# Attention of a macaron layer on one core: B and C scaled over all 128 partitions, M as one f32 product, and two orders at the tile's joints

## The chip, the core and the metric

The kernel runs on one core of a Trainium2 chip. The metric is the device time of one execution in microseconds (us). TensorE is PE in the rows (PEld its weight loads), VectorE is DVE, ScalarE is ACT, GpSimd is POOL, SyncE is SP.

## What is computed

A layer on x of 4 x 1024 tokens of 256 channels in f32: half a mixture-of-experts block (`f1`), an attention-like block (`at`), half the same mixture block again (`f2`), each on a layer norm of its input and added to it. The change concerns the middle block alone:

```python
xBC = x @ in_proj_w.T                       # 1024 of x, 1024 of z, 64 of B, 64 of C
xc = silu(conv4(xBC[..., :1024]) + conv_b)  # causal, 4 taps, per channel
step: h = h * exp(-exp(A)) + B_t * x_t ; y_t = sum_n h[n] * C_t[n]
yg = y * silu(z)
out = (layernorm(yg) * ln_w + ln_b) @ out_proj_w.T
```

The decay exp(-exp(A)) depends on the state number n alone (the 64 values are tested for being the same for all channels; the other way of computing is in the program and not taken).

## The kernel before

The 4096 tokens go through the middle block in 8 tiles of 512 tokens (t, 0 to 7; two tiles make one batch), each of four chunks of 128 (q, 0 to 3). The scan is done by chunks: with X the convolved x of a chunk, y = M X + (decayed C) S, where M is the masked product of B and C with the decay between two tokens in it, and S, the state at the chunk's start, takes in (decayed B) X at its end.

f32 products are made of three fast ones (`product`): a value is split into a rounded part (`_hi`, type F32R) and the remainder (`_lo`), and hi·hi + hi·lo + lo·hi are added. ScalarE rounds, VectorE (or GpSimd) subtracts.

Every engine has a written-out program, a function `tile(t, par)` in each engine's block with a loop over q, and semaphores between them; the order of work is the order of these programs. Work for tile t+1 (and t+2) is spread over the chunks of tile t:

- chunk 0: `project_bc` of t+1 on TensorE gives B and C in mm_ps, ScalarE copies them to `bc`, and GpSimd's `scale_bc` (L1180) multiplies by the table of decays `tab`, four operations: three give `g` and the fourth a half of `c_twice`.
- chunk 1: `round_g` on ScalarE (L1293, four casts), then `rest_of_g` on VectorE (L1466, three subtractions). VectorE also has `add_out` (L1504) here, which adds the output projection of the chunk before to x_res. It waits for that projection and for `res_biased`, GpSimd's addition of a bias to x_res (L1251), which GpSimd does in chunk 1 behind the power for the layer norm.
- chunk 2: `decays` on TensorE (L1686): four f32 products of g[:, 1] with `upper_twice` into one bank of mm_ps (for bo, the decayed B with tokens on partitions), then 24 products of 64 x 64 on 64 partitions into the other (M). ScalarE and VectorE split bo and mask M behind it.
- chunk 3: `transpose_xn` of tile t+2, and `rest_of_xT`.

`project_x(t, par, j)` is the projection of x's channel block j (six matmuls of 512 columns) into bank j % 2 of mm_ps; blocks 2 to 7 of tile t+1 go with chunks 0 to 2 of tile t, blocks 0 and 1 of tile t+2 with chunk 3. `project_z` gives z in two halves into zy_ps, `transpose_x` brings the next chunk's convolved x into xu_ps as X; `round_X` and `rest_of_X` split it, and the next chunk begins with the product of bo and X. In xu_ps lies the output projection too, so the second four of the eight transposes of `transpose_x` wait for `add_out`:

```python
for j in tuple(range(SUB, CT)) + tuple(range(SUB)):
    if j == 0 and not (isinstance(c, int) and c < 2):
        pe.wait_ge(s["out_added"], c - 1)
```

The part of y that comes from the state takes two more matmuls a bank (L1820, L1821), but in the first chunk of a batch: `c_twice` (128 partitions) against `S_split` (on partitions 64 to 127 the rounded S, on 0 to 63 its remainder), and the remainder of C, `g1_lo[HALF:P]`, on 64 partitions.

## Time and profile before

| what | us |
|---|---|
| median of 3 runs | 1633.81 (1628.12 to 1636.24) |
| span of the profiled execution | 1630.1 |
| `f1` / attention with its prologue / `f2`, in the profile | 0 to 484 / 484 to 1148 / from 1148 |
| a tile of the attention part | about 75 |

The page gives no time of the profiled execution beside its span; the three runs lie from 2.0 below to 6.1 above that span. In rows, a line number L is that of the kernel above; "out<-in" names the tiles, "x" the count of instructions, and brackets the engine's idle time before an instruction and what ended it. Successive matmuls overlap, so that the distance between their starts, not their duration, says what one costs.

### The profile page before, as it was taken

Reading aid. Unit: us, or ns where it says so; the run is one execution under the profiler, and the core shown is the slowest. Engines: PE = TensorE matmul, PEld = TensorE weight load, DVE = VectorE, ACT = ScalarE, POOL = GpSimd, SP = SyncE. Lnnn points to the kernel's source line nnn. Section 1 sums busy time; section 2 is a strip of 40 time slices with the busy share of each in tenths; the row PEclk is TensorE's granted clock in tenths of the full one; section 3 lists DMA queues with packets and bytes.
Section 4 is the critical chain, followed back from the end, with each engine's and each line's share of the span. In section 5 each row is a group of like instructions: output and inputs, shape, how many; then the busy total and the mean of one; then the engine's idle time right before and its main releaser. Section 6 shows DMA issues by size and latency. Waiting matters only on the chain. (4 is left out here: it accounts for less than half of the span.)

```text
span 1630.1 us, 24068 instructions
## 1 busy us (share of the span) xinstructions
PE 1408.4 (86%) x7430; PEld 1203.1 (74%) x7430; DVE 900.3 (55%) x2136; ACT 712.2 (44%) x1168; POOL 982.9 (60%) x1026
## 2 busy tenths in 40 slices
PE   6869999999926789999998999997597899999994
PEld 5758888888814667777776777776576788888883
DVE  5655323645446676676767576654476342255544
ACT  4323444444304455554545555543343244444430
POOL 2678447737455476676758576732147753773746
PEclk9989999999967789998999999899589899999997
DMA  9936667767343001000000000000712565777743
GB/s 370 388 108 217 212 219 258 268 230 266 120 151 102 1 1 30 23 27 14 27 14 28 14 27 1 27 27 1 290 53 97 197 228 201 262 252 248 262 149 123
DMA packets 90245, 225.46 MB, mean 138 GB/s; under 512 B 16640, under 2 KB 28928, under 8 KB 89216
## 3 DMA queue, kind: packets, MB, share of 16 engines
q1 hardware_dynamic: 65536, 156.64, 27.0%
q0 software_dynamic: 24576, 67.14, 12.6%
q8 instruction: 72, 1.18, 0.3%
q14 instruction: 61, 0.50, 0.1%
HBM read 114.67 MB, written 109.05 MB: 137 GB/s over the span
## 5 line engine op out<-in xcount | busy, mean ns | idle before, releaser
L374 POOL DMA_INDIRECT xg<-f_xn,f_rows x256 | 253.7, 991 | 185.5 <-issue 70.9
L401 POOL DMA_INDIRECT f_gbuf<-yg,f_rows x256 | 264.6, 1034 | 155.6 <-DMA yg<-f_yo 78.6
L809 PE MATMUL f_gu_ps<-f_wgu,f_xT 128*128 x1408 | 333.0, 379 | 0.0
L809 PEld LDWEIGHTS f_gu_ps<-f_wgu,f_xT 128*128 128x128 f32 x1408 | 253.8, 190 | 27.2
L840 PE MATMUL f_y_ps<-f_wd,f_hT 128*128 (+1 forms) x960 | 241.7, 380 | 4.9 <-DVE f_hT L636 4.8
L840 PEld LDWEIGHTS f_y_ps<-f_wd,f_hT 128*128 128x128 f32 x960 | 181.7, 190 | 32.6 <-issue 8.3
L628 DVE TENSOR_TENSOR f_h<-f_gu_ps,f_sg 128x256 f32<-128x256 f32 x176 | 74.6, 424 | 232.8 <-ACT f_sg L441 232.4
L428 ACT COPY f_xT<-f_xT_ps 128x512 f32<-128x512 f32 x232 | 136.0, 586 | 119.6 <-PE f_xT_ps L777 107.9
L654 DVE SCALAR_TENSOR_TENSOR f_xin<-f_gbuf,f_w,f_xin 128x256 f32<-128x256 f32 x256 | 124.1, 485 | 60.0 <-DMA f_gbuf<-yg,f_rows 53.1
L441 ACT ACTIVATE f_sg<-f_gu_ps 128x256 f32<-128x256 f32 x176 | 67.6, 384 | 201.0 <-PE f_gu_ps L809 201.0
L451 ACT COPY f_yo<-f_y_ps 128x512 f32<-128x512 f32 x176 | 103.2, 586 | 91.4 <-PE f_y_ps L840 91.4
L777 PE MATMUL f_xT_ps<-ident,f_xq 128*128 128x128 f32 x704 | 106.7, 275 | 34.8 <-DMA f_xq<-xg 31.8
L814 PE MATMUL f_gu_ps<-f_xT,f_wgu 128*128 128x256 f32 x512 | 130.6, 413 | 3.8 <-DVE f_hT L632 3.8
L1492 DVE SCALAR_TENSOR_TENSOR at_xs<-at_raw,at_taps,at_xs 128x512 f32<-128x512 f32 x132 | 113.9, 865 | 13.0 <-POOL at_xs L1210 9.4
L814 PEld LDWEIGHTS f_gu_ps<-f_xT,f_wgu 128*128 128x128 f32 x512 | 104.8, 210 | 20.0 <-issue 4.4
L1243 POOL TENSOR_TENSOR at_S_split<-at_S,at_S_split 64x1024 fp32r<-64x1024 f32 x32 | 77.6, 2425 | 53.1 <-ACT at_S_split L1389 53.1
L777 PEld LDWEIGHTS f_xT_ps<-ident,f_xq 128*128 128x128 f32 x704 | 82.9, 142 | 35.9 <-DMA f_xq<-xg 32.1
L1718 PE MATMUL at_xu_ps<-at_wout,at_ynT_hi 128*128 128x256 f32 x512 | 106.8, 308 | 2.4 <-DVE at_ynT_lo L1501 2.4
L1209 POOL TENSOR_SCALAR at_tap<-at_raw,at_taps 128x512 f32<-128x512 f32 x60 | 99.1, 1652 | 6.0
L636 DVE COPY f_hT<-f_hT_ps 128x256 f32<-128x256 f32 x176 | 74.5, 423 | 40.4 <-PE f_hT_ps L824 40.4
L1718 PEld LDWEIGHTS at_xu_ps<-at_wout,at_ynT_hi 128*128 128x128 f32 x512 | 89.0, 212 | 6.3 <-issue 2.9
L1654 PE MATMUL at_mm_ps<-at_xT_hi,at_win_hi 128*128 128x512 f32 x160 | 70.5, 441 | 20.1 <-ACT at_xs L1313 16.4
(234 smaller groups left out, 2742.2 us busy)
## 6 DMA issues: line engine op xcount, KB each, us to landing
f_xq<-xg SPq DMA_DIRECT2D x88, 512.0 KB, 4.6
yg<-f_yo SPq DMA_DIRECT2D x176, 256.0 KB, 2.7
xg<-f_gbuf SPq DMA_DIRECT2D x32, 512.0 KB, 16.5
f_wgu<-in_gate_up SPq DMA_DIRECT2D x4, 1280.0 KB, 21.5
f_xin<-in_x SPq DMA_DIRECT2D x8, 512.0 KB, 7.0
xg<-f_xn,f_rows POOLq DMA_INDIRECT x256
f_gbuf<-yg,f_rows POOLq DMA_INDIRECT x256
x<-f_xin SPq DMA_DIRECT2D x8, 512.0 KB, 3.6
```

The source lines that it names most:

```text
L374: G.indirect_dma_start(xg[g], bass.IndirectOffsetOnAxis(ap=rows[g][:, b, k:k + 1], axis=0), xn[:, SUB * TILE0[g] + b, :], None, bounds_che ...
L401: G.indirect_dma_start(gbuf[:, n % GBUF, k, :], None, yg[g], bass.IndirectOffsetOnAxis(ap=rows[g][:, b, k:k + 1], axis=0), bounds_check=2 ...
L428: A.copy(xT[:, k % 2], xT_ps[:, k % 2]).then_inc(xT_ready, 1)
L451: A.copy(yo[:, n % YO, :], y_ps[:, yy % 2]).then_inc(y_out, 1)
L654: ins = V.scalar_tensor_tensor(out=xin[:, n // SUB, n % SUB, :], in0=gbuf[:, n % GBUF, k, :], scalar=w4[g][:, b, k:k + 1], in1=xin[:, n // ...
L777: last = T.transpose(xT_ps[:, k % 2, c:c + P], of[s][:, d * P:(d + 1) * P], ident[:])
L809: last = T.matmul(gu_ps[:, j % 2, s * 2 * P:(s + 1) * 2 * P], x_of(k, s, d), weight(wgu[:, :, d, :], experts[s]), start=(d == 0), stop=(d ...
L814: last = T.matmul(gu_ps[:, j % 2, half * 2 * P:(half + 1) * 2 * P], wgu[:, experts[0], d, half * P:(half + 1) * P], xT[:, k % 2, 2 * d * P ...
L840: last = T.matmul(y_ps[:, yy % 2, s * D:(s + 1) * D], hT[:, i % 4, s * P:(s + 1) * P], weight(wd, experts[i][s]), start=(i == units[0]), s ...
L1209: link(G.tensor_scalar(tap0[:], raw[:, j % 2, 0:TILE], taps[:, j, 0:1], None, ALU.mult))
L1492: ins = V.scalar_tensor_tensor(out=acc, in0=raw[:, j % 2, k:k + TILE], scalar=taps[:, j, k:k + 1], in1=acc, op0=ALU.mult, op1=ALU.add)
L1718: nc.tensor.matmul(xu_ps[:, 0, 0:D], ynT_hi[:, j, :], wout[:, j, i, :], start=(j == 0 and i == 0), stop=False)
```

## The change

Four things.

1. **B and C over 128 partitions.** The input projection's weights are laid out as B, B, C, C (before B, C, C, B), so that `bc[:, 0]` holds B twice, on both halves of the partitions, and `bc[:, 1]` C twice. `tab` has four full tables, `scale_bc` gives four full `g` of 128 partitions (f32). g[:, 0] and g[:, 1] are B and C scaled for M, one half of the partitions each for one half of the chunk's tokens, with zeros in the table where they don't apply; g[:, 2] is B for bo, g[:, 3] C for y. The constant `upper_twice` goes.
2. **No splitting for M and bo.** `decays` makes four transposes of g[:, 2] and four plain f32 products of 128 x 128 of g[:, 0] and g[:, 1], on 128 partitions. `round_g` is one cast (`c_twice`), `rest_of_g` one subtraction (`c_rest`), and the product of C's remainder with S is over 128 partitions. `decays` waits for `g_ready` as well.
3. **VectorE, chunk 1**: `add_out` stands ahead of `rest_of_g`.
4. **TensorE, chunk 3**: `project_x(t + 2, par, 1, ...)` stands ahead of `transpose_x` where there is a tile two on.

```diff
-    g = sb("g", [P, 3, TILE])
-    g1_hi = sb("g1_hi", [P, 2, TILE], F32R)
-    g1_lo = sb("g1_lo", [P, 2, TILE], F32R)
+    g = sb("g", [P, 4, TILE])
     c_twice = sb("c_twice", [P, 2, TILE], F32R)
-    g23_hi = sb("g23_hi", [P, 2, TILE], F32R)
-    g23_lo = sb("g23_lo", [P, 2, TILE], F32R)
+    c_rest = sb("c_rest", [P, 2, TILE], F32R)
...
         def scale_bc(t, par, parts=range(4)):
             pool.wait_ge(s["bc_copied"], 2 * (t + 1))
             for i in parts:
-                k, n = ((0, P), (1, P), (0, HALF), (1, HALF))[i]
-                to = g[0:n, i, :] if i < 3 else c_twice[0:HALF, par, :]
-                G.tensor_tensor(to.rearrange("p (q t) -> p q t", q=SUB),
-                                bc[0:n, k, :].rearrange("p (q t) -> p q t", q=SUB),
-                                tab[0:n, i, :].unsqueeze(1).broadcast_to([n, SUB, P]), ALU.mult).then_inc(s["g_ready"], 1)
+                G.tensor_tensor(g[:, i, :].rearrange("p (q t) -> p q t", q=SUB),
+                                bc[:, i % 2, :].rearrange("p (q t) -> p q t", q=SUB),
+                                tab[:, i, :].unsqueeze(1).broadcast_to([P, SUB, P]), ALU.mult).then_inc(s["g_ready"], 1)
...
         def round_g(t, par):
             act.wait_ge(s["g_ready"], 4 * (t + 1))
-            A.copy(g1_hi[:, par, :], g[:, 0, :]).then_inc(s["g_hi_ready"], 1)
-            A.copy(g23_hi[:, 0, :], g[:, 1, :]).then_inc(s["g_hi_ready"], 1)
-            A.copy(g23_hi[0:HALF, 1, :], g[0:HALF, 2, :]).then_inc(s["g_hi_ready"], 1)
-            A.copy(c_twice[HALF:P, par, :], g[HALF:P, 0, :]).then_inc(s["g_hi_ready"], 1)
+            A.copy(c_twice[:, par, :], g[:, 3, :]).then_inc(s["g_hi_ready"], 1)
...
         def rest_of_g(t, par):
-            dve.wait_ge(s["g_hi_ready"], 4 * (t + 1))
-            for i in range(3):
-                gh_, gl_, n = ((g1_hi[:, par, :], g1_lo[:, par, :], P), (g23_hi[:, 0, :], g23_lo[:, 0, :], P),
-                               (g23_hi[:, 1, :], g23_lo[:, 1, :], HALF))[i]
-                V.tensor_tensor(gl_[0:n], g[0:n, i, :], gh_[0:n].bitcast(F32), ALU.subtract).then_inc(s["g_lo_ready"], 1)
+            dve.wait_ge(s["g_hi_ready"], t + 1)
+            V.tensor_tensor(c_rest[:, par, :], g[:, 3, :], c_twice[:, par, :].bitcast(F32), ALU.subtract).then_inc(s["g_lo_ready"], 1)
...
+                    if q == 1:
+                        add_out(t, c - 1, q - 1)
                     if q == 1 and more(t, 1):
                         rest_of_g(t + 1, nx)
-                    if q == 1:
-                        add_out(t, c - 1, q - 1)
...
             pe.wait_ge(s["raw_ready"], CT * t + (CT if isinstance(t, int) and t == 0 else 6))
-            pe.wait_ge(s["g_lo_ready"], 3 * (t + 1))
+            pe.wait_ge(s["g_ready"], 4 * (t + 1))
+            pe.wait_ge(s["g_lo_ready"], t + 1)
             for q in range(SUB):
-                last = nc.tensor.matmul(mm_ps[:, 0, q * P:(q + 1) * P], g[:, 1, q * P:(q + 1) * P], upper_twice[:],
-                                        start=True, stop=True)
+                last = nc.tensor.transpose(mm_ps[:, 0, q * P:(q + 1) * P], g[:, 2, q * P:(q + 1) * P], ident[:])
             last.then_inc(s["bo_in_psum"], 1)
             for q in range(SUB):
                 a = q * P
-                for blk in range(2):
-                    b_hi = g1_hi[0:HALF, par, a:a + P] if blk == 0 else g23_hi[0:HALF, 1, a:a + P]
-                    b_lo = g1_lo[0:HALF, par, a:a + P] if blk == 0 else g23_lo[0:HALF, 1, a:a + P]
-                    t0 = a + blk * HALF
-                    last = product(mm_ps[:, 1, t0:t0 + HALF], b_hi, b_lo, g23_hi[0:HALF, 0, t0:t0 + HALF],
-                                   g23_lo[0:HALF, 0, t0:t0 + HALF], True, True)
+                last = nc.tensor.matmul(mm_ps[:, 1, a:a + P], g[:, 0, a:a + P], g[:, 1, a:a + P], start=True, stop=True)
             last.then_inc(s["m_in_psum"], 1)
...
-                            last = nc.tensor.matmul(y_ps[:, n, :], g1_lo[HALF:P, par, ca], S_split[HALF:P, cols],
+                            last = nc.tensor.matmul(y_ps[:, n, :], c_rest[:, par, ca], S_split[:, cols],
                                                     start=False, stop=True)
...
                 elif more(t, 1):
                     project_z(c + 1, nx, 0, 1)
+                    if more(t, 2):
+                        project_x(t + 2, par, 1, "xT_lo_ready", t + 3)
                     transpose_x(t + 1, c + 1, nx, 0)
...
-                if q == 3 and more(t, 2):
-                    project_x(t + 2, par, 1, "xT_lo_ready", t + 3)
```

Three places show the moves. On VectorE, chunk 1 of a tile, from the convolution to the split of X (L1471 is `rest_of_g`, L1507 `add_out`), before:

```order
L1492 SCALAR_TENSOR_TENSOR at_xs<-at_raw,at_taps,at_xs 128x512 x2
L1471 TENSOR_TENSOR at_g_lo<-at_g,at_g_hi 128x512 x2
L1471 TENSOR_TENSOR at_g_lo<-at_g,at_g_hi 64x512
L1507 TENSOR_TENSOR at_x_res<-at_xu_ps,at_x_res 128x256
L1554 TENSOR_TENSOR at_X_lo<-at_xu_ps,at_X_hi 128x1024
L1501 TENSOR_TENSOR at_ynT_lo<-at_zy_ps,at_ynT_hi 128x1024
```

and now (L1456 is `rest_of_g`, L1492 `add_out`):

```order
L1477 SCALAR_TENSOR_TENSOR at_xs<-at_raw,at_taps,at_xs 128x512 x2
L1492 TENSOR_TENSOR at_x_res<-at_xu_ps,at_x_res 128x256
L1456 TENSOR_TENSOR at_c_rest<-at_g,at_c_twice 128x512
L1539 TENSOR_TENSOR at_X_lo<-at_xu_ps,at_X_hi 128x1024
L1486 TENSOR_TENSOR at_ynT_lo<-at_zy_ps,at_ynT_hi 128x1024
```

`add_out` has moved ahead, and of three subtractions one is left.

On TensorE, chunk 2 of tile 0, from the last product of y to the output projection, before (the three rows of 128x64 stand there eight times in all):

```order
L1821 MATMUL at_y_ps<-at_S_split,at_g_lo 128x512
L1809 UNCONDITIONAL_BRANCH
L1691 MATMUL at_mm_ps<-at_upper_twice,at_g 128x128 x4
L1654 MATMUL at_mm_ps<-at_g_hi 128x64
L1655 MATMUL at_mm_ps<-at_g_lo,at_g_hi 128x64
L1656 MATMUL at_mm_ps<-at_g_hi,at_g_lo 128x64
```

and now:

```order
L1799 MATMUL at_y_ps<-at_S_split,at_c_rest 128x512
L1787 UNCONDITIONAL_BRANCH
L1675 MATMUL at_mm_ps<-ident,at_g 128x128 x4
L1679 MATMUL at_mm_ps<-at_g 128x128 x4
L1696 MATMUL at_xu_ps<-at_wout,at_ynT_hi 128x256 x2
```

The 24 products of 64 columns have become one row of four, and the products with `upper_twice` are transposes.

On TensorE, end of tile 0, from the last matmul of z to the transposes of yn, before (L1743 is `transpose_x`, the six behind it `project_x` of block 1, L1709 `transpose_yn`):

```order
L1656 MATMUL at_zy_ps<-at_win_hi,at_xT_lo 128x512
L1743 MATMUL at_xu_ps<-ident,at_xs 128x128 x8
L1654 MATMUL at_mm_ps<-at_xT_hi,at_win_hi 128x512
L1655 MATMUL at_mm_ps<-at_xT_lo,at_win_hi 128x512
L1656 MATMUL at_mm_ps<-at_xT_hi,at_win_lo 128x512
L1654 MATMUL at_mm_ps<-at_xT_hi,at_win_hi 128x512
L1655 MATMUL at_mm_ps<-at_xT_lo,at_win_hi 128x512
L1656 MATMUL at_mm_ps<-at_xT_hi,at_win_lo 128x512
L1709 MATMUL at_zy_ps<-ident,at_yn 128x128 x8
```

and now (L1721 is `transpose_x`, L1687 `transpose_yn`):

```order
L1639 MATMUL at_zy_ps<-at_win_hi,at_xT_lo 128x512
L1637 MATMUL at_mm_ps<-at_xT_hi,at_win_hi 128x512
L1638 MATMUL at_mm_ps<-at_xT_lo,at_win_hi 128x512
L1639 MATMUL at_mm_ps<-at_xT_hi,at_win_lo 128x512
L1637 MATMUL at_mm_ps<-at_xT_hi,at_win_hi 128x512
L1638 MATMUL at_mm_ps<-at_xT_lo,at_win_hi 128x512
L1639 MATMUL at_mm_ps<-at_xT_hi,at_win_lo 128x512
L1721 MATMUL at_xu_ps<-ident,at_xs 128x128 x8
L1687 MATMUL at_zy_ps<-ident,at_yn 128x128 x8
```

The six matmuls have changed places with the eight transposes of X.

## Rows read from the trace of the kernel before

**Rows 1.** Windows view of the attention part: us, busy us (count) by engine, PEclk, DMA, GB/s.

```profile
554.00:1124.00 570.00, 519.37 (x2752) 422.12 (x2751) 374.62 (x546) 292.34 (x383) 377.03 (x366) 0.95 0.06 19
```

**Rows 2.** Waits view of TensorE, 561 to 1124 us: total, times, longest.

```profile
PE at_xu_ps L1743 <- DVE at_x_res L1507: 29.5, 8, 4.4
```

**Rows 3.** Timeline, tile 2, chunk 1, TensorE, VectorE, GpSimd: start, us, what, [idle before].

```profile
737.51 0.60 PE L1743 MATMUL at_xu_ps<-ident,at_xs 128*128 128x128 f32 x4
...
741.93 1.11 PE L1743 MATMUL at_xu_ps<-ident,at_xs 128*128 128x128 f32 x4 [3.82 <-DVE at_x_res L1507]
...
737.49 4.04 DVE L1471 TENSOR_TENSOR at_g_lo<-at_g,at_g_hi 128x512 fp32r<-128x512 f32 x3
...
741.47 0.41 DVE L1507 TENSOR_TENSOR at_x_res<-at_xu_ps,at_x_res 128x256 f32<-128x256 f32 x1
...
737.58 2.81 POOL L1251 TENSOR_TENSOR at_x_res<-at_x_res,at_bias_out 128x1024 f32<-128x1024 f32 x1
```

**Rows 4.** Timeline, tile 7, chunk 1, GpSimd and TensorE.

```profile
1106.79 2.35 POOL L1251 TENSOR_TENSOR at_x_res<-at_x_res,at_bias_out 128x1024 f32<-128x1024 f32 x1
...
1109.72 1.11 PE L1743 MATMUL at_xu_ps<-ident,at_xs 128*128 128x128 f32 x4 [2.38 <-DVE at_x_res L1507]
```

**Rows 5.** Timeline of TensorE, tile 3, chunk 0.

```profile
786.76 0.40 PE L1655 MATMUL at_xu_ps<-at_X_lo,at_bo_hi 128*128 128x512 f32 x1
...
787.93 0.40 PE L1654 MATMUL at_y_ps<-at_X_hi,at_m_hi 128*128 128x512 f32 x1
...
791.28 0.40 PE L1655 MATMUL at_mm_ps<-at_xT_lo,at_win_hi 128*128 128x512 f32 x1
```

**Rows 6.** Timeline of VectorE, tile 2, chunk 3.

```profile
775.27 1.22 DVE L1464 TENSOR_TENSOR at_xT_lo<-at_mm_ps,at_xT_hi 128x1024 fp32r<-128x1024 f32 x1 [0.33 <-ACT at_xT_hi L1286]
```

**Rows 7.** Timeline of TensorE, tile 2: chunk 2, then an output projection in chunk 0.

```profile
753.02 1.16 PE L1691 MATMUL at_mm_ps<-at_upper_twice,at_g 128*128 128x128 f32 x8
...
754.11 0.29 PE L1654 MATMUL at_mm_ps<-at_g_hi 64*128 64x64 f32 x1
...
756.90 0.51 PE L1718 MATMUL at_xu_ps<-at_wout,at_ynT_hi 128*128 128x256 f32 x2
...
761.37 0.39 PE L1654 MATMUL at_mm_ps<-at_xT_hi,at_win_hi 128*128 128x512 f32 x1
...
717.20 0.40 PE L1718 MATMUL at_xu_ps<-at_wout,at_ynT_hi 128*128 128x256 f32 x2
...
720.02 0.40 PE L1654 MATMUL at_mm_ps<-at_xT_hi,at_win_hi 128*128 128x512 f32 x1
```

**Rows 8.** Windows view, inside the output projection at 756.90.

```profile
757.70:761.10 3.40, 3.40 (x18) 3.40 (x17) 2.05 (x4) 1.24 (x1) 1.16 (x2) 0.50 0.01 2
```

**Rows 9.** Timeline, tile 2, chunk 2, VectorE, ScalarE, TensorE.

```profile
761.57 0.42 DVE L1507 TENSOR_TENSOR at_x_res<-at_xu_ps,at_x_res 128x256 f32<-128x256 f32 x1 [1.79 <-PE at_xu_ps L1719]
...
759.08 1.24 ACT L1332 ACTIVATE at_yn<-at_yn,at_ynb,at_yrstd 128x1024 f32<-128x1024 f32 x1 [3.90 <-POOL at_ynb L1248]
...
767.82 1.04 PE L1709 MATMUL at_zy_ps<-ident,at_yn 128*128 128x128 f32 x8
```

**Rows 10.** Timeline of VectorE, prologue.

```profile
539.41 2.30 DVE L1471 TENSOR_TENSOR at_g_lo<-at_g,at_g_hi 128x512 fp32r<-128x512 f32 x3
...
549.26 0.72 DVE L1482 COPY_PREDICATED at_m_full<-at_causal,at_mm_ps 128x512 f32<-128x512 int32 x1 [2.01 <-PE at_mm_ps L1656]
```

**Rows 11.** Timeline, end of tile 1, TensorE and ScalarE.

```profile
706.06 1.03 PE L1743 MATMUL at_xu_ps<-ident,at_xs 128*128 128x128 f32 x8
...
709.03 1.09 PE L1709 MATMUL at_zy_ps<-ident,at_yn 128*128 128x128 f32 x8 [0.54 <-ACT at_sz L1337]
...
711.53 0.49 PE L1654 MATMUL at_xu_ps<-at_X_hi,at_bo_hi 128*128 128x512 f32 x1 [1.41 <-DVE at_X_lo L1554]
...
707.96 1.02 ACT L1337 ACTIVATE at_sz<-at_zy_ps 128x1024 f32<-128x1024 f32 x1
...
708.86 1.02 ACT L1328 CAST at_X_hi<-at_xu_ps 128x1024 fp32r<-128x1024 f32 x1
```

More of the change, by code:

```diff
@@ L987, in attn_block @@
     pick = sb("pick", [P, 2])
-    upper_twice = sb("upper_twice", [P, P])
     names = """rate_ready w_in0 w_in1 small_in rate_in a_in ga_in w_out w_hi w_lo w_lo_v init_p init_v init_a x_in ln_read var_ready rstd_ready
@@ L1020, in attn_block @@
     bcg = scratch["bc_rows"]
-    INIT_P = 19
+    INIT_P = 17
     block = ctx.enter_context(nc.Block())
@@ L1151, in _ @@
         make(G.memset(expo[lo, 0, HALF:P], 0.0))
-        make(G.iota(expo[hi, 0, :], [[1, P]], base=1, **kw))
-        make(G.iota(expo[lo, 1, :], [[0, 2], [1, HALF]], base=-(HALF // 2), **kw))
-        make(G.iota(expo[hi, 1, :], [[-1, P]], base=P - 1, **kw))
-        make(G.iota(expo[lo, 2, :], [[-1, P]], base=HALF + HALF // 2, **kw))
-        make(G.memset(expo[hi, 2, :], 0.0))
-        make(G.iota(expo[lo, 3, :], [[1, P]], base=1, **kw))
-        make(G.memset(expo[hi, 3, :], 0.0))
+        make(G.iota(expo[hi, 0, :], [[-1, P]], base=HALF + HALF // 2, **kw))
+        make(G.iota(expo[lo, 1, 0:HALF], [[1, HALF]], base=-(HALF // 2), **kw))
+        make(G.memset(expo[lo, 1, HALF:P], 0.0))
+        make(G.memset(expo[hi, 1, 0:HALF], 0.0))
+        make(G.iota(expo[hi, 1, HALF:P], [[1, HALF]], base=-(HALF // 2), **kw))
+        make(G.iota(expo[:, 2, :], [[-1, P]], base=P - 1, **kw))
+        make(G.iota(expo[:, 3, :], [[1, P]], base=1, **kw))
         make(G.memset(half_neg[:], -0.5))
         make(G.memset(zeros[:], 0.0))
-        make(G.memset(upper_twice[:], 0.0))
-        make(G.affine_select(out=upper_twice[:].rearrange("p (i n) -> p i n", i=2),
-                             in_=upper_twice[:].rearrange("p (i n) -> p i n", i=2), compare_op=ALU.not_equal, fill=1.0,
-                             base=-HALF, pattern=[[0, 2], [-1, HALF]], channel_multiplier=1))
         make(G.memset(m_full[:], 0.0))
@@ L1220, in _ @@
         rstd_of(1)
-        pool.wait_ge(s["init_a"], 4)
+        pool.wait_ge(s["init_a"], 5)
         pool.wait_ge(s["small_in"], 64)
@@ L1229, in _ @@
         pool.wait_ge(s["w_lo_v"], 3)
-        pool.wait_ge(s["init_a"], 8)
+        pool.wait_ge(s["init_a"], 9)
         first_tap(1, 1, 0)
@@ L1275, in _ @@
         act.wait_ge(s["init_a"], 2)
-        A.mul(tab[0:HALF, 0, HALF:P], ones[0:HALF, 0:HALF], 0.0).then_inc(s["init_a"], 1)
+        A.mul(tab[0:HALF, 0:2, HALF:P], ones[0:HALF, 0:P].rearrange("p (i t) -> p i t", i=2), 0.0).then_inc(s["init_a"], 1)
+        A.mul(tab[HALF:P, 1, 0:HALF], ones[HALF:P, 0:HALF], 0.0).then_inc(s["init_a"], 1)
         A.activation(chunk_decay[:], rate[:], ACT.Exp, scale=float(P)).then_inc(s["init_a"], 1)
@@ L1341, in _ @@
         A.activation(ga[:], ga[:], ACT.Exp).then_inc(s["init_a"], 1)
-        act.wait_ge(s["init_a"], 5)
+        act.wait_ge(s["init_a"], 6)
         A.activation(ga[:], ga[:], ACT.Exp, scale=-1.0).then_inc(s["init_a"], 1)
@@ L1525, in _ @@
         link(V.tensor_reduce(flag_f[:, 0:1], S[:, 0:CT * NST], AX.X, ALU.max))
-        dve.wait_ge(s["init_a"], 7)
+        dve.wait_ge(s["init_a"], 8)
         link(V.tensor_scalar(sz[:, NST:2 * NST], sz[:, NST:2 * NST], MAX_RATE, None, ALU.is_gt))
@@ L1579, in tile @@
                     dve.wait_ge(s["gbc_in"], 16 * (c + 1))
-                    link(V.tensor_copy(gb[0:HALF, :], gbc[0:HALF, 0, :]))
-                    link(V.tensor_copy(gb[HALF:P, :], gbc[HALF:P, 1, :]))
-                    link(V.tensor_copy(gc[0:HALF, :], gbc[0:HALF, 1, :]))
-                    link(V.tensor_copy(gc[HALF:P, :], gbc[HALF:P, 0, :]))
+                    link(V.tensor_copy(gb, gbc[:, 0, :]))
+                    link(V.tensor_copy(gc, gbc[:, 1, :]))
                     if first:
@@ L1776, in _ @@
             project_x(1, 1, j, "xT_lo_ready", 2)
-        pe.wait_ge(s["init_a"], 8)
+        pe.wait_ge(s["init_a"], 9)
         pe.wait_ge(s["w_lo_v"], 3)
@@ L1928 @@
     w_in = i[attn + "in_proj_w"]
-    w_in = np.concatenate([w_in, w_in[COL_BC + NST:COL_BC + 2 * NST], w_in[COL_BC:COL_BC + NST]])
+    w_b, w_c = w_in[COL_BC:COL_BC + NST], w_in[COL_BC + NST:COL_BC + 2 * NST]
+    w_in = np.concatenate([w_in[:COL_BC], w_b, w_b, w_c, w_c])
     halves = (SH, P, D)
```

## The prediction

> **What bounds the kernel now.** I first read the windows view of the attention part, the only part that the diff touches. From 554 to 1124 us TensorE is busy for 519 of 570 us while VectorE has 375, GpSimd 377 and ScalarE 292, and its mean granted clock is 0.95 [rows 1]. So TensorE's own work is the path, cut by a few waits and by stretches at half clock. The waits view then names the largest cut: 29.5 us in 8 waits, once a tile, of the transposes of X for `add_out` on VectorE [rows 2]. The other waits of TensorE there are at the tiles' ends.
>
> The timeline of tile 2 shows that wait in chunk 1 [rows 3]. TensorE issues four transposes at 737.51 and the other four at 741.93, after 3.82 us idle. VectorE runs the three subtractions of `rest_of_g` for 4.04 us from 737.49 and only then `add_out`, 0.41 us at 741.47. It looks as if the three subtractions were the whole cause. They are not: `add_out` has a second semaphore, `res_biased`, which GpSimd's addition of the bias to x_res (L1251) gives, and that addition runs from 737.58 to 740.39.
>
> **The change part by part.** (a) **add_out ahead of rest_of_g.** TensorE resumes 741.93 − 740.39 = 1.54 us after the bias addition ends. In the last tile, where no `rest_of_g` stands between, it resumes 1109.72 − (1106.79 + 2.35) = 0.58 us after [rows 4]. That is 0.96 us won. The bias addition itself took 2.35 us there against 2.81 beside the subtractions: 0.45 more. So 1.41 us in each of tiles 0 to 6, 9.9 us in all, not the 3.8 of the wait. Bounds: 0.96 (the addition stays at 2.81) to 3.8 (the wait goes). Late next is GpSimd's chain: taps, the remainder of S, the power, the bias. Behind the waiting `add_out` are `rest_of_g` and `rest_of_X`; the latter waits for transposes that wait for the same thing, so nothing is lost. `decays`, which needs c_rest, is over 10 us later.
>
> (b) **The remainder of C over 128 partitions instead of 64.** Matmuls of 512 columns start every 0.234 us (786.76 to 787.93, five steps). From 787.93 to 791.28 there are eleven steps, 3.35 us, where full ones would take 2.57 [rows 5]: the two 64-partition products and the change to and from them cost 0.78 us a chunk. The change makes them like their neighbours. 28 of 32 chunks have them (not the first of each batch). Where it counts: chunk 2 of 8 tiles, 6.2 us. In chunk 3 VectorE has its own queue ahead of the remainder of xT, and waited there for only 0.33 us [rows 6]: 0.33 × 8 = 2.6. In chunks 0 and 1 it only brings TensorE to the wait of (a) earlier, unless GpSimd is released earlier too: in odd tiles by chunk 0 (3 × 0.78 = 2.3), in the last tile, where GpSimd has little else, by both (1.6). Together 12.7 of a possible 28 × 0.78 = 21.8.
>
> (c) **decays.** Before, the four products for bo start at 753.02, the 24 small ones at 754.11, and the next work at 756.90: 3.88 us [rows 7]. After: four transposes, at most the 0.60 of the four in [rows 3], I take 0.4; four f32 products of 128 x 128, which is the form of the four at 753.02, so 754.11 − 753.02 = 1.09; and 0.1 for the change of kind. 1.6 us, a gain of 2.3 in each of tiles 0 to 6: 16.0. The f32 product of M costs no more than bo's did, because the operands' types and sizes are the same; bounds 0.8 and 2.2. Here a rule speaks against the change. The Trainium skill, "FP8 and Floating Point Precision", section "TensorE Precision Notes", says that true FP32 makes four passes through the array: four passes of 128 columns, four times, are 2,048 columns, where the 24 small products are 1,536. If columns set the price, M would get a third dearer. The trace disagrees: the small ones cost 2.79/24 = 0.116 us for 64 columns, half of what 512 columns take.
>
> (d) **The clock after decays.** The output projection that follows takes 761.37 − 756.90 = 4.47 us, in another chunk 720.02 − 717.20 = 2.82 [rows 7], and in between the granted clock is 0.50 [rows 8], that is 1.2 instead of 2.4 GHz, after a run of small products without any idle time. They are gone, so I take 1.6 × 7 = 11.2 us. Nothing in the trace shows the clock behind the new sequence; bounds 0 and 1.6 a tile.
>
> (e) **What chunk 2 can take.** (b), (c) and (d) bring TensorE 0.78 + 2.3 + 1.6 = 4.7 us forward there. `add_out` was waiting 1.79 us for TensorE at 761.57, so VectorE is free from 759.8; the second four transposes would want it by about 759.9, and it takes 0.42. ScalarE ends normalize_y at 760.32, then has the copies of block 6 (about 1.1), X_hi and the silu of z (1.0 each, as in [rows 11]) to do, till about 763.4, where the transposes of yn would start at 767.82 − 4.7 = 763.1 [rows 9]. So some 0.4 us of the 4.7 is given back: −2.8 us over seven tiles.
>
> (f) **Casts and subtractions taken away.** Three of four casts on ScalarE and two of three subtractions on VectorE hide: ScalarE waits for GpSimd behind them. Only in the prologue is it serial: three subtractions in 2.30 us become one of 0.7, and the mask waited 2.01 us for the small products [rows 10]: 3.6 us. GpSimd's four multiplications of B and C keep their count and columns: nothing. The new wait of `decays` for `g_ready` is met long before.
>
> (g) **The projection ahead of the transposes at the tile's end**, six times. The transposes of tile 1's end start at 706.06 and end at 707.09; with six matmuls ahead of them (6 × 0.234 = 1.4) they end at 708.5. Their reader, X_hi, starts at 708.86, because ScalarE has the silu of z from 707.96 [rows 11]. So they stay just hidden, by 0.4 us. What ended TensorE's two waits, 0.54 for sz and 1.41 for X_lo, is that chain of ScalarE, which comes from VectorE's convolution, and no order on TensorE shortens it. Worth 0; bounds +1.0 a tile (the hidden 0.4 is lost and the rest shows) and −0.3.
>
> The sum: 9.9 + 12.7 + 16.0 + 11.2 − 2.8 + 3.6 + 0 = 50.6 us. The profiled execution's span is 1630.1; 1630.1 − 50.6 = 1579.5. The median of the runs shown, 1633.8, is 3.7 above that span, so the time is 1583 us, 3.1% less.
>
> **Rivals.** *The wait goes altogether.* The diff's order suggests it: remove the 3 us that I leave of it in each of seven tiles, and the half-clock stretch behind it (741.93's transposes took 1.11 for four, against 0.60), some 1.5 each: 31 us more, 1552. Against it stands GpSimd's end at 740.39.
>
> *The clock stays down behind decays,* since four-fold f32 products are not what the neighbours are: (d) falls away, 1594; if it also stays down for longer behind the shortened wait, 1.6 × 7 more, 1605.
>
> *M's price by columns* (the four passes named under c, as a mechanism of this kernel: M 2.79 × 2048/1536 = 3.7 instead of 1.1, 2.6 × 7 = 18 us): 1601.
>
> *The tile end becomes later* (g at its upper bound, and chunk 2 gives back 1 us instead of 0.4): 6 + 4 = 10 us, 1593.
>
> *Slower than before: TensorE's clock through the whole loop.* The gain leaves a 3 us wait in a tile that has 7 us less of TensorE's work, and the clock has answered such waits. Each us at half level costs half a us, so it decides from 101 us of half clock more than now, 14 in each of seven tiles; with 24 more in each it would be 84 − 51 = 33 us slower, 1667. For it: half level followed the wait of tile 2, and waits will take a larger share of a shorter tile; against it: the mean over the part is 0.95 now, with longer waits [rows 1].
>
> *The change does not do what it says:* the order rows show that all three moves are in the program.
>
> **How the numbers follow.** My forecast, 1573 to 1592: 0.52. Clock down behind decays: 0.12. Later tile end or fuller chunk 2: 0.11. Columns' price: 0.05. The wait gone, or much more of it than I say: 0.13. Full gain lost to something in other waits, within 0.5% of before: 0.04. Slower: 0.03. From 1562 to 1603 lie the first four cases (0.80) but for their ends; the bounds of (a), (c) and (d) lie within it. A measurement of this kernel can tell 0.5%, 8 us, from no change. Faster 0.93, same 0.04, slower 0.03.
>
> **What would show it.** In the changed profile: the transposes of X in chunk 1 still wait for `add_out`, about 3 us, and VectorE's `add_out` now waits for GpSimd's bias addition, which takes 2.35 to 2.4 us; `decays` takes 1.6 us; the output projection behind it takes 2.8 at granted clock 1; the matmuls of y start every 0.234 us; the tile's end waits 0.5 and 1.4 us as before. A tile takes 68 us instead of 75. I am wrong on (a) if that wait is under 1.5 us, on (d) if the clock is still 0.5 behind `decays`, on (g) if X_hi waits for the transposes at a tile's end.

## The result, and the profile after

The changed kernel takes 1593.42 us (median of 4 runs, 1591.58 to 1595.43), the kernel before, in the same session, 1632.18 us (4 runs, 1628.12 to 1636.24). The ratio is 0.9763, with a 95% interval of 0.9743 to 0.9784: 2.4% less time. Forecast were 1583 us and a range of 1562 to 1603. So the sign and the range held, and the gain was smaller than the sum: the profiled span went from 1630.1 to 1593.7 us, 36.4 less, where the terms gave 50.6. By the medians it is 38.8 less (the profiled run of the changed kernel, 1595.43, is its slowest), so what is missing is 12 to 14 us. This part follows it, as the 14.2 of the profiled spans.

First the page of the changed kernel, its busy times and the granted clock in 40 slices, and then the windows view of the attention part, which answers to [rows 1].

```profile
span 1593.7 us, 23708 instructions
...
PE 1368.9 (86%) x7270; PEld 1184.2 (74%) x7270; DVE 881.4 (55%) x2120; ACT 698.8 (44%) x1145; POOL 971.1 (61%) x1024
...
PEclk9988999999986689999999999998598999999997
```

```profile
545.00:1105.00 560.00, 502.11 (x2700) 421.58 (x2700) 369.44 (x547) 290.12 (x373) 370.63 (x370) 0.93 0.06 19
```

TensorE has less to do, but its mean granted clock over the attention part is 0.93, against 0.95 before, although the half clock behind `decays` should be gone. The waits view of TensorE from 530 to 1090 us (total, times, longest) says where it now stands still:

```profile
PE at_xu_ps L1721 <- DVE at_x_res L1492: 21.7, 8, 2.9
PE at_zy_ps L1687 <- ACT at_sz L1325: 17.7, 10, 3.2
PE at_xu_ps L1637 <- DVE at_X_lo L1539: 8.1, 7, 1.4
```

The first row was 29.5 us [rows 2]. The second is mostly a wait at the tile's end, for the silu of z (sz in the rows). I had left it at 0.54 us a tile.

**Chunk 1 of tile 2**, which answers to [rows 3]: TensorE, VectorE, GpSimd.

```profile
731.42 0.66 PE L1721 MATMUL at_xu_ps<-ident,at_xs 128*128 128x128 f32 x4 [2.82 <-DVE at_x_res L1492]
...
730.94 0.42 DVE L1492 TENSOR_TENSOR at_x_res<-at_xu_ps,at_x_res 128x256 f32<-128x256 f32 x1 [2.45 <-POOL at_x_res L1241]
731.28 0.68 DVE L1456 TENSOR_TENSOR at_c_rest<-at_g,at_c_twice 128x512 fp32r<-128x512 f32 x1
...
728.49 2.34 POOL L1241 TENSOR_TENSOR at_x_res<-at_x_res,at_bias_out 128x1024 f32<-128x1024 f32 x1
```

`add_out` (L1492) no longer waits for its place on VectorE but for GpSimd's bias addition (L1241), for 2.45 us. That addition takes 2.34 us. TensorE resumes at 731.42, 0.59 us after its end at 730.83. Those are the forecast's 2.35 and 0.58, and the wait that it left, "about 3 us", is 2.82.

**`decays` and the output projection behind it**, tile 2, TensorE, and the windows view over both; they answer to [rows 7, 8].

```profile
740.89 0.60 PE L1675 MATMUL at_mm_ps<-ident,at_g 128*128 128x128 f32 x4
741.33 1.06 PE L1679 MATMUL at_mm_ps<-at_g 128*128 128x128 f32 x8
742.14 0.48 PE L1696 MATMUL at_xu_ps<-at_wout,at_ynT_hi 128*128 128x256 f32 x2
...
745.05 0.39 PE L1637 MATMUL at_mm_ps<-at_xT_hi,at_win_hi 128*128 128x512 f32 x1
```

```profile
738.00:745.60 7.60, 7.60 (x53) 6.87 (x52) 7.07 (x9) 3.68 (x6) 5.75 (x5) 1.00 0.01 2
```

From 740.89 to 742.14 `decays` takes 1.25 us instead of 3.88: 0.44 for the four transposes (bo), 0.81 for the four f32 products of M. Each of these products stands in the profile as two MATMUL rows, so that the row of L1679 says x8. The output projection takes 745.05 − 742.14 = 2.91 us instead of 4.47, and the clock stays at 1.00.

**The end of tile 2** is where the forecast failed. TensorE and ScalarE answer to [rows 11]; VectorE and GpSimd are shown for what they do at that time; the last fence is the windows view behind it.

```profile
765.58 1.03 PE L1721 MATMUL at_xu_ps<-ident,at_xs 128*128 128x128 f32 x8
768.50 1.09 PE L1687 MATMUL at_zy_ps<-ident,at_yn 128*128 128x128 f32 x8 [1.89 <-ACT at_sz L1325]
770.92 0.79 PE L1637 MATMUL at_xu_ps<-at_X_hi,at_bo_hi 128*128 128x512 f32 x1 [1.33 <-DVE at_X_lo L1539]
...
774.08 0.63 PE L1638 MATMUL at_y_ps<-at_X_lo,at_m_hi 128*128 128x512 f32 x1
...
762.00 2.58 DVE L1477 SCALAR_TENSOR_TENSOR at_xs<-at_raw,at_taps,at_xs 128x512 f32<-128x512 f32 x2
...
762.75 1.29 POOL L1181 TENSOR_TENSOR at_m_lo<-at_m_full,at_m_hi 128x512 fp32r<-128x512 f32 x1
...
764.62 0.63 ACT L1306 ACTIVATE at_xs<-at_xs 128x512 f32<-128x512 f32 x1 [4.75 <-DVE at_xs L1477]
...
767.43 1.02 ACT L1325 ACTIVATE at_sz<-at_zy_ps 128x1024 f32<-128x1024 f32 x1
768.33 1.02 ACT L1316 CAST at_X_hi<-at_xu_ps 128x1024 fp32r<-128x1024 f32 x1
```

```profile
768.50:777.90 9.40, 8.07 (x26) 6.32 (x27) 5.34 (x6) 3.16 (x5) 4.42 (x6) 0.64 0.00 0
```

Read the wait for sz first: 1.89 us, not 0.54. Then the two taps of the convolution on VectorE: 2.58 us for two. In the kernel before, at the same place (end of tile 3), they took 1.53, and GpSimd's subtraction for the remainder of M came only as they ended:

```profile
778.56 1.53 DVE L1492 SCALAR_TENSOR_TENSOR at_xs<-at_raw,at_taps,at_xs 128x512 f32<-128x512 f32 x2
...
780.10 1.28 POOL L1191 TENSOR_TENSOR at_m_lo<-at_m_full,at_m_hi 128x512 fp32r<-128x512 f32 x1
...
781.04 1.03 PE L1743 MATMUL at_xu_ps<-ident,at_xs 128*128 128x128 f32 x8
```

Now it starts 0.75 us into them. Both engines read two operands from SBUF, and the convolution takes 1.05 us more. ScalarE's silu of x (L1306) waits for it, and behind that on ScalarE stand sz and X_hi. Last, the granted clock: 0.64 over the 9.4 us behind the transposes of yn, and products of 512 columns take 0.63 us each instead of 0.40 (they start 0.43 apart instead of 0.23). The trace's record of the granted clock has half level for 6.8 us at the end of each of tiles 0 to 5, the first from 626.9, the last from 981.9. Before, there was none there (the windows view over 9.4 us from the transposes of yn at tile 2's end, in the kernel before, follows), but one behind each `decays`; that one is gone. Behind the wait of chunk 1 there was half clock before and there is now.

```profile
784.05:793.45 9.40, 8.08 (x35) 5.74 (x36) 7.70 (x7) 5.16 (x7) 6.06 (x6) 1.00 0.01 2
```

From the end of tile 0 to that of tile 6 (from TensorE's first product there to the same product six tiles on) a tile takes 70.4 us on average, 1050.92 − 628.79 = 422.1 us for six, where 68 was forecast and about 75 stood before (448.7 for six). In these six tiles the record holds 47.8 us of half clock before and 56.2 now. This time for six tiles is the measure used below beside the whole time, because it leaves out what differs ahead of the tiles and behind them from one execution to the next.

So two things happened at the tile's end that the forecast held at nothing: a collision of GpSimd with the convolution, and half clock. The third part of the change, the projection ahead of the transposes, acts at the same place. The experiments take them apart.

### The profile page after: what moved, and what is told of

The parts are those of the page before. It is cut to its first block and busy times, and to the rows that moved or that the text cites. A ratio compares the mean times of both kernels' runs of the same rounds, so it can differ in the third digit from the quotient of the medians.

```text
span 1593.7 us, 23708 instructions
## 1 busy us (share of the span) xinstructions
PE 1368.9 (86%) x7270; PEld 1184.2 (74%) x7270; DVE 881.4 (55%) x2120; ACT 698.8 (44%) x1145; POOL 971.1 (61%) x1024
## 5 line engine op out<-in xcount | busy, mean ns | idle before, releaser
L814 PEld LDWEIGHTS f_gu_ps<-f_xT,f_wgu 128*128 128x128 f32 x512 | 103.4, 207 | 19.3 <-issue 4.4
L1696 PE MATMUL at_xu_ps<-at_wout,at_ynT_hi 128*128 128x256 f32 x512 | 95.1, 286 | 2.4 <-DVE at_ynT_lo L1486 2.4
L1200 POOL TENSOR_TENSOR at_xs<-at_xs,at_tap 128x512 f32<-128x512 f32 x60 | 83.9, 1399 | 5.0
L1637 PE MATMUL at_mm_ps<-at_xT_hi,at_win_hi 128*128 128x512 f32 x160 | 69.1, 432 | 18.6 <-ACT at_xs L1301 14.5
```

Of the source, the lines that this page charges most:

```text
L814: last = T.matmul(gu_ps[:, j % 2, half * 2 * P:(half + 1) * 2 * P], wgu[:, experts[0], d, half * P:(half + 1) * P], xT[:, k % 2, 2 * d * P ...
L1696: nc.tensor.matmul(xu_ps[:, 0, 0:D], ynT_hi[:, j, :], wout[:, j, i, :], start=(j == 0 and i == 0), stop=False)
```

## The experiments

The theory after the result: the 14 us that are missing lie at the tile's end, and half clock there makes most of them. Its rivals were: the collision alone costs them; the order alone costs them; or the sum was wrong elsewhere.

**1 and 2. The projection back behind the transposes, in the changed kernel.** Experiment 2 is the same edit again, beside a repetition of the changed kernel.

```diff
-                    if more(t, 2):
-                        project_x(t + 2, par, 1, "xT_lo_ready", t + 3)
...
+                if q == 3 and more(t, 2):
+                    project_x(t + 2, par, 1, "xT_lo_ready", t + 3)
```

> The changed kernel with only the move on TensorE undone (the projection behind the transposes again). Theory (collision): in the changed kernel the last convolution of a tile takes 2.58 us instead of 1.53 because GpSimd's rest_of_m now runs beside it, ScalarE's chain is late by that, TensorE waits 1.89 and 1.33 us at the tile's end, and the half-clock stretch of 6.8 us that begins there follows from that waiting; the order on TensorE has no part in it. Then: waits 1.9 and 1.3, half clock at six tiles' ends, 1593 us. Rival (order): the half clock comes from the transposes of X lying directly against the waits, with no projection between them; then the waits are the same, the half clock at the tiles' ends is gone, and the time is 20 us less, 1573.

Measured: 1579.39 us (4 runs, 1575.59 to 1582.88), against 1631.43 for the kernel before on that chip: 0.9673, 0.9641 to 0.9705. The profiled span is 1579.2 us; the forecast's sum for the whole change had been 1579.5. Of the two theories written down, the one by which the order has no part in it (1593) is refuted; the other had given 1573. TensorE in tile 2's end, and the windows view over the same 9.4 us from the transposes of yn:

```profile
758.07 1.09 PE L1721 MATMUL at_xu_ps<-ident,at_xs 128*128 128x128 f32 x8 [0.95 <-ACT at_xs L1306]
758.92 0.48 PE L1637 MATMUL at_mm_ps<-at_xT_hi,at_win_hi 128*128 128x512 f32 x1
...
761.27 1.09 PE L1687 MATMUL at_zy_ps<-ident,at_yn 128*128 128x128 f32 x8 [0.71 <-ACT at_sz L1325]
763.68 0.50 PE L1637 MATMUL at_xu_ps<-at_X_hi,at_bo_hi 128*128 128x512 f32 x1 [1.32 <-DVE at_X_lo L1539]
```

```profile
761.27:770.67 9.40, 8.08 (x39) 6.59 (x40) 7.66 (x7) 5.33 (x8) 6.62 (x7) 1.00 0.00 0
```

The waits add up to 0.95 + 0.71 + 1.32 = 2.98 us here and to 3.22 in the changed kernel: the order hardly changes how long TensorE stands still. The collision is there too:

```profile
754.77 2.58 DVE L1477 SCALAR_TENSOR_TENSOR at_xs<-at_raw,at_taps,at_xs 128x512 f32<-128x512 f32 x2
...
755.52 1.28 POOL L1181 TENSOR_TENSOR at_m_lo<-at_m_full,at_m_hi 128x512 fp32r<-128x512 f32 x1
```

What differs is the clock: 39 products in the 9.4 us against 26. The six tiles take 410.5 us instead of 422.1, with 19 us of half clock instead of 56. So the order costs about 14 us in this kernel, 11.6 of the 14.5 between the profiled spans in these six tiles, and through the clock, not through waiting. Another 2.6 lie ahead of tile 0's end, where the changed kernel's record has one stretch of 6.8 us more, at 572.3; its repetition doesn't have it. The repetition:

> The changed kernel as it is, to have it on the same chip as the next three. 0.976 of the kernel before, half clock of 6.8 us at six tiles' ends, waits of 1.89 and 1.3 us there.

> x1 once more beside the changed kernel. Theory (order and collision together bring the half clock): 14 us less than x9 in the same call, no half clock at the tiles' ends but one. Rival: x1's gain was the chip or the placing of the clock's stretches in that run; then within 5 us of x9.

Measured: the changed kernel 1593.69 us (0.9764, 0.9745 to 0.9783), without the order 1581.95 us (0.9689, 0.9668 to 0.971), before 1632.15. The difference is 11.7 us here, and for the six tiles 421.1 against 410.1. Half clock stood again at the ends of tiles 0 to 5 of the one and at none of them of the other. At tile 6's end, where both kernels have the same order (there is no tile two on), both have 6.8 us of it.

**3. GpSimd's remainder of M behind its first taps**, which takes the collision away and leaves the order.

```diff
-                if q == 3 and more(t, 1):
-                    rest_of_m(t + 1, nx)
...
+                if q == 3 and more(t, 1):
+                    rest_of_m(t + 1, nx)
```

> The changed kernel with GpSimd's rest_of_m in chunk 3 behind the first tap of the tile two on, instead of ahead of it. Theory (collision): the last convolution takes 1.53 again, TensorE's wait for sz at the tile's end falls from 1.89 to about 0.9, the clock stays full there, 1593 - 6 x (1.0 + 3.4) = 1567 us. Rival (order): the wait is 0.9, the half clock stays, 1593 - 6 = 1587. Third: the longer convolution is not GpSimd's doing, 2.58 and 1593 stay.

Measured: 1580.13 us (0.9671, 0.9638 to 0.9703). The convolution takes 1.53 us again, and the wait for sz is 0.84:

```profile
755.60 1.53 DVE L1477 SCALAR_TENSOR_TENSOR at_xs<-at_raw,at_taps,at_xs 128x512 f32<-128x512 f32 x2
...
762.38 1.28 POOL L1181 TENSOR_TENSOR at_m_lo<-at_m_full,at_m_hi 128x512 fp32r<-128x512 f32 x1
...
761.05 1.09 PE L1687 MATMUL at_zy_ps<-ident,at_yn 128*128 128x128 f32 x8 [0.84 <-ACT at_sz L1325]
```

This came out between what the two theories gave (1567 and 1587). The collision's removal shortens the tile's end by 1 us and, with it, half clock is left at two of the six ends, for 3.4 us each. But GpSimd's chain still sets when the bias addition ends, so part of what the tile's end gained came back as a longer wait in chunk 1: 3.11 us instead of 2.82 in tile 2, 24.9 instead of 21.7 over all tiles.

**4. Both undone.**

> Both: rest_of_m later and the move on TensorE undone. Theory (collision): as x2 within 2 us, 1567. Rival (order): wait 0.9 and clock full, 1567 too, but then x1 is at 1573 and x2 at 1587; the four times (changed, x1, x2, x3) tell the two apart.

Measured: 1580.4 us (0.9687, 0.966 to 0.9714). Either edit gives 13 to 14 us, both together no more. They are not two costs that add up. Half clock at all six ends was seen only where the longer wait and the projection's absence between the two groups of transposes came together. Half clock is left at two ends here, where experiment 1 has none, so the agreement with 1567 that both theories asked for failed by 13 us.

**5 and 6. Each move alone, in the kernel before.** These two and the next two ran on a chip where the kernel before takes 1913.45 us (1909.25 to 1924.44, 14 runs), where the parts before and behind attention take longer. Their times are compared only with the kernel before on that chip. First only `add_out` ahead of `rest_of_g`:

```diff
+                    if q == 1:
+                        add_out(t, c - 1, q - 1)
                     if q == 1 and more(t, 1):
                         rest_of_g(t + 1, nx)
```

> The kernel before with only add_out put ahead of rest_of_g. Theory (GpSimd's bias addition bounds add_out): TensorE's wait in chunk 1 falls from 3.6 to 3.8 us to about 2.3, VectorE now waits for the bias addition, which takes 2.35 instead of 2.8; 7 x 1.4 = 10 us less, 1621. Rival (the subtractions were the whole wait): 27 us less or more, 1600.

Measured: 1905.0 us, 0.9946 (0.9918 to 0.9974): 8.5 us less by the medians, 5 to 16 by the interval. The wait for `add_out` is still 1.7 to 3.0 us. Term (a) was 9.9.

Then only the projection ahead of the transposes:

> The kernel before with only the projection put ahead of the transposes at a tile's end. Theory (the order costs the clock only where the waits behind it are long): the waits stay 0.54 and 1.3 us, rest_of_m does not meet the last convolution (1.53 us), no half clock at the tiles' ends, 1631 us within 4. Rival (the order alone makes the clock fall): six half-clock stretches at the tiles' ends, 10 to 20 us more, 1641 to 1651.

Measured: 1915.02 us, 0.9999 (0.9969 to 1.003). The waits at the tile's end stay 0.54 and 1.3 (in tile 3 they add up to 2.0, as before), and no half clock follows them in tiles 0 to 5, though 3.8 us lie there between the last product and the next. By itself, in the kernel before, the third part of the change costs nothing that can be measured (the interval is 6 us to either side), just as forecast; it costs 12 to 14 us beside the other two.

**7. The changed kernel with both orders as before**, so with the wide g alone.

> The changed kernel with both orders undone: only the 128 partitions and the unsplit M. Theory: rest_of_g is one operation of 0.7 us and fits in while GpSimd adds the bias, so that it matters little which stands first; the time is x1's, 1580 within 4 us, of the kernel before 51 less. Rival: the contention with the bias addition costs 0.45 us a tile and is answered by the clock, 1580 + 3 to 10.

Measured: 1869.62 us, 0.9765 (0.9737 to 0.9792): 43.8 us less. Terms (b) to (f) add up to 40.7. Written down beforehand was 51 less, the gain of experiment 1; that missed by 7. With `rest_of_g` down to one subtraction, the wait for `add_out` is 3.4 us in tiles 1, 2, 3 and 5, and 2.8 to 2.95 with `add_out` ahead. So even then the order is worth some 0.5 us a tile: the six tiles take 413.3 us here and 410.5 in experiment 1, which differs in this order alone, but ran on another chip. That is 2.8 of the 7 to 8; the rest isn't settled.

**8. The bias addition in two pieces**, the first as large as what `add_out` of chunk 0 touches.

```diff
-                    G.tensor_tensor(x_res[:], x_res[:], bias_out[:].unsqueeze(1).broadcast_to([P, SUB, D]),
+                    G.tensor_tensor(x_res[:, 0, :], x_res[:, 0, :], bias_out[:], ALU.add).then_inc(s["res_biased"], 1)
+                    G.tensor_tensor(x_res[:, 1:SUB, :], x_res[:, 1:SUB, :], bias_out[:].unsqueeze(1).broadcast_to([P, SUB - 1, D]),
...
-            dve.wait_ge(s["res_biased"], t + 1)
+            dve.wait_ge(s["res_biased"], 2 * t + (1 if q == 0 else 2))
```

> The changed kernel with only the bias addition in two. Theory: the wait in chunk 1 falls to about 1.2 us and the half clock behind it goes, as in x4; at the tile's end the convolution still takes 2.58, the wait 1.89 and the half clock stays: 1593 - 7 x (1.6 + 1.7) = 1570, that is 14 more than x4. Rival: what matters in x4 is the bias addition alone, and x8 is at x4's 1556.

Measured: 1845.53 us, 0.9657 (0.9605 to 0.9708). The wait in chunk 1 falls to 0.9 to 1.3 us in all tiles but the first, and the half clock behind it goes. At the tile's end the waits stay, 1.89 and 1.3 us, and half clock comes at all six ends, for 6.8 us at four and for 3.4 at the other two. Written down was 1570 where the changed kernel takes 1593; the ratio makes it 1576 there, an estimate. Tile 2, from the transposes of yn:

```profile
892.80:902.20 9.40, 8.06 (x26) 6.37 (x27) 5.44 (x6) 3.23 (x5) 4.42 (x5) 0.64 0.00 0
```

These are the same 26 products in 9.4 us. So what happens at the tile's end does not come from chunk 1's wait.

**9 to 11. The pieces put together.** The split bias with the remainder of M later:

> x2 and in addition GpSimd's bias addition in two operations, the first 128 x 256 alone releasing the add_out of chunk 1. Theory: add_out waits for GpSimd and for nothing else, so TensorE's wait in chunk 1 falls from 2.8 to about 1.0 us (the 2.35 us operation becomes one of about 0.65), the half clock behind it (3.4 us in seven tiles) goes too: 7 x 1.7 + 6 x 1.7 = 22 us less than x2, 1545. If the clock stays: 12 less, 1555. Rival: add_out is bound by TensorE's own projection or by VectorE; no gain over x2.

Measured: 1556.34 us (5 runs, 1549.59 to 1557.85), 0.954 (0.9515 to 0.9566). GpSimd's two pieces and TensorE's return in tile 2, and the 9.4 us behind the transposes of yn:

```profile
713.12 0.72 POOL L1241 TENSOR_TENSOR at_x_res<-at_x_res,at_bias_out 128x256 f32<-128x256 f32 x1
713.80 1.84 POOL L1242 TENSOR_TENSOR at_x_res<-at_x_res,at_bias_out 128x768 f32<-128x768 f32 x1
...
713.87 0.42 DVE L1493 TENSOR_TENSOR at_x_res<-at_xu_ps,at_x_res 128x256 f32<-128x256 f32 x1 [0.76 <-POOL at_x_res L1241]
...
714.35 0.66 PE L1722 MATMUL at_xu_ps<-ident,at_xs 128*128 128x128 f32 x4 [1.23 <-DVE at_x_res L1493]
```

```profile
748.80:758.20 9.40, 8.05 (x40) 6.58 (x41) 7.63 (x7) 5.37 (x8) 7.84 (x8) 1.00 0.00 0
```

`add_out` is released by the 0.72 us of the first piece, and the record of the clock has no half level from 580 us to the last tile. With that, 1545 had been expected, and 1555 only if half clock stayed. The profiled run is the fastest of the five (1549.59, the others 1555.76 to 1557.85, with a mean clock of 0.937 to 0.938 instead of 0.940), so its trace may show less half clock than the others had, and its 385.9 us for the six tiles in the table below are likely too low for its median. The split bias with the projection back behind the transposes:

> x8 (bias addition in two) with the move on TensorE undone, the collision left. Theory: half clock gone in chunk 1 by the split and at the tiles' ends by the order; the late ScalarE chain still costs about 1 us a tile: x4 and 3 to 6 us, some 1560 on a chip where before is 1632. Rival: with the chunk-1 wait short TensorE meets the tile's end as x8 did and the half clock stays, 1570.

Measured: 1565.34 us (0.959, 0.957 to 0.9609), in the middle between the two expectations. All three edits:

> x4 with the move on TensorE undone: bias addition in two, rest_of_m later, old order. Theory: in x4 no half clock was left in the loop, so the order has nothing more to give or take: as x4 within 3 us, 0.954 of before. Rival: the projection ahead of the transposes is worth its 1.4 us of cover in a fast loop, and this is up to 1 us a tile slower than x4, 6 us.

Measured: 1555.63 us (1554.97 to 1557.26), 0.9539 (0.9521 to 0.9557), the same as experiment 9. So with the bias addition split and the collision gone, the order on TensorE no longer matters. Experiments 9 and 11 are the fastest versions found: 76 us below the kernel before, 38 below the changed one.

| kernel | us | ratio to before (95%) | waits at tile 2's end, us | from the last product to the next, us | ends of tiles 0 to 5 with half clock | six tiles, us |
|---|---|---|---|---|---|---|
| before | 1632.18 | 1 | 0.54, 1.32 | 3.0 | 0 | 448.7 |
| changed | 1593.42 | 0.9763 (0.9743 to 0.9784) | 1.89, 1.33 | 5.2 | 6, of 6.8 us | 422.1 |
| changed, again | 1593.69 | 0.9764 (0.9745 to 0.9783) | 1.89, 0.61 (transposes of yn at half clock) | 5.2 | 6, of 6.8 us | 421.1 |
| 1 order undone | 1579.39 | 0.9673 (0.9641 to 0.9705) | 0.71, 1.32 | 3.1 | 0 | 410.5 |
| 2 the same, again | 1581.95 | 0.9689 (0.9668 to 0.971) | 0.71, 1.31 | 3.1 | 0 | 410.1 |
| 3 remainder of M later | 1580.13 | 0.9671 (0.9638 to 0.9703) | 0.84, 1.34 | 4.1 | 2, of 3.4 us | 410.8 |
| 4 both | 1580.4 | 0.9687 (0.966 to 0.9714) | 0.71, 1.32 | 3.1 | 2, of 3.4 us | 410.0 |
| 6 before, with the projection ahead | 1915.02, other chip | 0.9999 (0.9969 to 1.003) | 0.54, 1.32 | 3.8 | 0 | 447.8 |
| 8 split bias alone | 1845.53, other chip | 0.9657 (0.9605 to 0.9708) | 1.89, 1.33 | 5.2 | 6: four of 6.8 us, two of 3.4 | 402.9 |
| 9 split bias, M later | 1556.34 | 0.954 (0.9515 to 0.9566) | 0.84, 1.33 | 4.1 | 0 | 385.9 |
| 10 split bias, order undone | 1565.34 | 0.959 (0.957 to 0.9609) | 0.71, 1.32 | 3.1 | 1, of 3.4 us | 396.1 |
| 11 split bias, M later, order undone | 1555.63 | 0.9539 (0.9521 to 0.9557) | 0.71, 1.31 | 3.1 | 2, of 3.4 us | 390.9 |

The fifth column, like the last, is worked out from TensorE's rows. In the changed kernel the last product ends with the start of the transposes of X, about 765.7, and the next starts at 770.92. With the order undone, six products stand between the two groups of transposes, and it is 3.1 us: 0.71, 1.09 for the transposes of yn, and 1.32. In the changed kernel the fall of the clock lies inside this stretch and not behind it: 3.1 us after the last product in tile 4, just as the transposes of yn begin (909.91; the fall is at 910.2), 4.6 us after it in tile 2. So in tile 4 the second wait had no part in the fall.

## Why the prediction was right or wrong

**(a) add_out ahead of rest_of_g: right**, mechanism and size. The second semaphore decided. In the changed trace `add_out` waits for the bias addition, which takes 2.34 us (forecast 2.35), and TensorE resumes 0.59 us behind it (0.58). Alone, the move brought 8.5 us (5 to 16) where 9.9 was written. The rival "the wait goes altogether" would have been 27 us there and is refuted.

**(c) and (d) decays and the clock behind it: right.** `decays` takes 1.25 us and not 1.6, some 2.4 us more gain over seven tiles than written; the output projection 2.91, not 2.8; the clock is 1.00. "M's price by columns" and "the clock stays down behind decays" both fall. The first would have M take 3.7 us; the four f32 products took 0.81 together, where the 24 small ones took 2.79. The step that failed in that rival is not the count of passes but the price of the small products. The Trainium skill, "FP8 and Floating Point Precision", section "TensorE Precision Notes", gives true FP32 four passes, which for one product of 128 columns makes 512 columns. The trace agrees in time (it shows two rows a product): 0.20 us a product, where a product of 512 columns costs 0.234. It is the small products that cost more than their columns, 0.116 us for 64.

**(b), (e), (f): right as a sum only.** They were not tried one by one. The products of y start every 0.234 us, as forecast. The terms (b) to (f), 40.7, stand beside the 43.8 of experiment 7. (e) itself did not come: in chunk 2 the transposes of yn start without idle time in every tile where the forecast had them wait (in tile 2 at 751.68, as the silu of z has ended at 751.51), so the 2.8 us were not given back. With that and the shorter `decays` the terms would add up to about 45. In (f), the mask of the prologue came at 546.99 us instead of 549.26, though the attention part began 1.3 us later: so 2.3 + 1.3 = 3.6 us within the part, as written.

**(g) the projection ahead of the transposes: wrong**, and this is the step that failed. I wrote: "So they stay just hidden, by 0.4 us." and "Worth 0; bounds +1.0 a tile". As an account of the waits it holds: their sum moved by 0.24 us between the orders, and in the kernel before the move cost nothing (0.9999). In the changed kernel it costs 11.7 to 14.0 us, above the upper bound of 6. It left out two things.

The first is whom the faster TensorE meets. Under (f) I costed GpSimd at nothing, since its work keeps its count and columns. But in each chunk VectorE and GpSimd now come to their work at other times relative to each other. At the tile's end the remainder of M came to lie upon the convolution, whose taps went from 1.53 to 2.58 us; ScalarE's chain hangs on it, and the two waits of TensorE went from 0.54 + 1.32 = 1.86 us to 1.89 + 1.33 = 3.22. The rule that bears on this is in the Trainium skill, "SBUF — State Buffer", section "Who interferes with whom": a VectorE instruction with two SBUF inputs contends with a GpSimd instruction that reads SBUF, and the order of issue decides who is blocked. By it, the second tap, which comes 0.03 us behind GpSimd's subtraction, would start as that ends, at 764.04, and last 0.75: an estimate of 764.8 for the end. The trace has 764.58, so it agrees with the rule in kind, and the estimate is 0.2 us too long. GpSimd's subtraction, which came first, keeps its time: 1.29 us against 1.28 before. I had read the same mechanism in [rows 3], where the bias addition took 2.81 beside the subtractions, and had used it for one pair of instructions only.

The second is what the projection was doing there besides its own work. It stood between TensorE's two groups of transposes, with a wait behind each. With it ahead, TensorE goes 5.2 us with nothing but 16 transposes and two waits, and half clock comes for 6.8 us at each end of tiles 0 to 5. With it back, or with the collision gone, that stretch is 3.1 to 4.3 us, and half clock came at 0 to 2 of the six ends, for 3.4 us. Over the six tiles the changed kernel has 56.2 us of half clock and experiment 1 has 19.3 (2.2 of them at tile 6's end, where the changed kernel has none). Half of the 36.9 between them, 18, is the most that can be lost by it; 11.6 was, since part of the half clock lies over waits and part of the loss is taken back by a shorter wait in chunk 1 (21.7 us in all against 24.4). In the repetition it was 11.0. So half clock at the tiles' ends makes 11 to 12 of the missing 12 to 14 us; what remains lies outside the six tiles, where one execution differs from the next by 2 to 3 us.

The rival "the tile end becomes later" gave the right time, 1593, for a wrong reason: it priced 1 us of plain lateness in each tile, not the clock. "TensorE's clock through the whole loop" had the right mechanism at a place it didn't name.

**What stays open.** Why half clock comes at some ends and not at others with the same waits (experiments 3, 4 and 11 have it at two of six, and 1 and 9 at none) isn't settled. Tile 6's end shows it best: there every kernel has the transposes together and three waits, 5.1 to 5.6 us between the products, and half clock came in 6 of the 14 traces. The changed kernel has none there and its repetition has 6.8 us. So the length of the stretch alone does not decide; what came before it may, but no run moves only that. Nor was (b) measured alone.

## What to carry to other kernels

Before a reorder is credited with a whole wait, read every semaphore on which the waiting instruction stands: here the second one left 2.8 of 3.8 us, and splitting the instruction that gives it, so that the first 0.72 us release the reader, was worth more than the reorder. When one engine gets faster, lay the new times of VectorE and GpSimd against each other at each place where a third engine waits for one of them; an instruction that keeps its cost alone may double it in new company. And matmuls that stand between two waits of TensorE can be what keeps its clock up: here moving them ahead cost nothing where the waits were short (experiment 6, and 9 against 11) and 12 to 14 us where they were 1.4 us longer. So read the granted clock behind a reorder, and not only the waits.
